# A pair-sum loop that takes in more of the next layer's work, on one Trainium2 core

## The reference

```
h   = tanh(txt_proj[:, None] + feat_proj[:, :, None] + b)
rho = h . w  + (1 - q_mask) * NEG
att = softmax(rho);  txt_h = att @ text
x   = x + tanh(g) * (tanh(txt_h . Wcw) * features + tanh(txt_h . Wcb))
```

## Time and profile before

| | us |
|---|---|
| median of 3 runs (lowest, highest) | 616.18 (615.16, 616.81) |
| the profiled execution | 613.41 |
| its span in the profile | 611.6 |
| PE busy, share of the span | 563.5, 92% |
| DVE | 445.4, 73% |
| ACT | 415.8, 68% |
| POOL | 117.0, 19% |

### The profile page before, as it was taken

How to read it: one execution, slowest core, us unless ns; L and a number is a source line. 1 busy time by engine, 2 the same in 40 slices (tenths; PEclk the granted TensorE clock), 3 DMA queues, 4 the chain that set the end, 5 groups by cost and what they waited for, 6 DMA issues and landing times.

```text
span 611.6 us, 8766 instructions
## 1 busy us (share of the span) xinstructions
PE 563.5 (92%) x3281; PEld 390.9 (64%) x3284; DVE 445.4 (73%) x684; ACT 415.8 (68%) x581; POOL 117.0 (19%) x74
## 2 busy tenths in 40 slices
PE   7999999978998999998865899999998999999997
PEld 5667887846776777776210247556655777788886
DVE  4358988768646889986968658576767836787786
ACT  4779888916754565656999976624504856988885
POOL 5400000241210000002999914200000310000000
PEclk9999999979999999999899999999999999999999
DMA  6207110200200811020000022604610110812100
GB/s 233 70 15 298 49 55 1 73 2 1 75 1 3 312 38 41 34 69 1 2 5 1 1 69 70 194 16 122 190 34 1 38 36 0 297 50 70 35 1 34
DMA packets 16782, 40.27 MB, mean 66 GB/s; under 512 B 1834, under 2 KB 6058, under 8 KB 16740
## 3 DMA queue, kind: packets, MB, share of 16 engines
q1 hardware_dynamic: 16740, 39.71, 19.5%
HBM read 39.01 MB, written 0.70 MB: 65 GB/s over the span
## 4 chain that ended last, share of the span: by engine, by line
PE 71%; DVE 13%; ACT 11%; issue 3%; POOL 1%; ACTq 0%; DVEq 0%; POOLq 0%
PE ps L680 38%; ACT work L1046 7%; PE ps L723 4%; DVE h_lo L1523 3%; PE ps L445 2%; PE ps L573 2%; PE ps L706 2%; PE ps L544 2%; PE ps L708 2%; PE ps L707 2%; PE ps L462 2%; PE ps L662 2%; PE ps L558 2%; PE ps L452 2%; PE ps L439 1%
## 5 line engine op out<-in xcount | busy, mean ns | idle before, releaser
L1523 DVE TENSOR_TENSOR h_lo<-h_act,h_hi 128x512 fp32r<-128x512 f32 (+1 forms) x136 | 120.0, 886 | 41.0 <-ACT h_hi L1083 40.4
L680 PE MATMUL ps<-n_hi,w_hi 128*128 128x512 f32 (+1 forms) x232 | 85.8, 403 | 6.8 <-DVE h_act L1500 4.3
L1083 ACT CAST h_hi<-h_act 128x1024 fp32r<-128x1024 f32 (+1 forms) x88 | 75.3, 856 | 15.3 <-PE ps L680 12.8
L680 PE MATMUL ps<-n_hi,w_lo 128*128 128x512 f32 (+1 forms) x232 | 83.1, 392 | 0.0
L680 PE MATMUL ps<-n_lo,w_hi 128*128 128x512 f32 (+1 forms) x232 | 83.0, 391 | 0.0
L1721 POOL TENSOR_TENSOR rstd<-var_eps,minus_half 128x4 f32<-128x4 f32 x16 | 17.8, 1114 | 313.5 <-DVE var_eps L1217 313.5
L680 PE MATMUL ps<-h_hi,w_hi 128*128 128x512 f32 (+1 forms) x184 | 65.6, 399 | 4.5 <-DVE h_lo L1523 4.3
L680 PE MATMUL ps<-h_hi,w_lo 128*128 128x512 f32 (+1 forms) x184 | 64.3, 392 | 0.0
L680 PE MATMUL ps<-h_lo,w_hi 128*128 128x512 f32 (+1 forms) x184 | 64.0, 390 | 0.0
L1046 ACT ACTIVATE work<-work,p_rest 128x2048 f32<-128x2048 f32 x32 | 61.4, 2000 | 1.3 <-DVE work L1388 1.3
L1755 POOL TENSOR_TENSOR work<-xc,txt 128x2048 f32<-128x2048 f32 x16 | 58.3, 3684 | 5.0 <-ACT xc L1023 4.3
(11 more groups left out here) (225 smaller groups left out, 1015.9 us busy)
## 6 DMA issues: line engine op xcount, KB each, us to landing
work<-g_rows SPq DMA_DIRECT2D x36, 512.0 KB, 6.5
w_f<-in_w SPq DMA_DIRECT2D x20, 512.0 KB, 3.5
w_f<-in_w SPq DMA_DIRECT2D x8, 544.0 KB, 3.7
work<-in_w SPq DMA_DIRECT2D x2, 512.0 KB, 4.5
work<-g_rows SPq DMA_DIRECT2D x4, 256.0 KB, 9.2
p_rest<-in_p_rest SPq DMA_DIRECT2D x1, 714.0 KB, 9.9
p_attn<-in_p_attn SPq DMA_DIRECT2D x1, 546.5 KB, 7.0
x<-in_xT SPq DMA_DIRECT2D x1, 512.0 KB, 3.7
```

The source lines that it names most:

```text
L680: mm = pe.matmul(dst[i], wap(wt, e, lo, size, rows), mv[i], start=(first and c == 0), stop=(last and c == 2))
L1083: act.copy(places(h_hi, m, step), places(h_act, m, step)).then_inc(s["hi"], 1)
L1523: dve.tensor_tensor(lo, src, hi.bitcast(F32), ALU.subtract).then_inc(s["lo"], 1)
```

## The change

- **Sums.** POOL gets the even groups from 2 to 30 (15), DVE group 0 and all odd ones (17). Group 0's sum is made in two halves of 16 features, and so is its tanh. PE makes the features of half 0 twice, into bank 2 (read by DVE) and bank 0 (copied by ACT); group 0's sum waits for the first of the two alone.
- **Mask.** The mask bias is put into the dots' bank by a PE product with the identity ahead of each half's dots; DVE's addition is gone.
- **Finish.** Both last products of the MoE before are finished by DVE at g = 3.
- **Fourth layer.** Values (all) and keys of half 0 are made in the loop by PE and copied by DVE instead of ACT; keys of half 1 move to steps 5 and 8 of the MoE, with ACT copies at its steps 19 and 22.
- **Next MoE.** Softmax, weights, update and norm (5, 0) of half 0 stand earlier in the loop. norm_high, the logits, the routing's activation (as Exp, with an addition and a reciprocal on DVE) and up(0), up(1) are in the loop, and DVE routes half 0 ahead of softmax(1). Behind the loop the order on PE, ACT and DVE is new.

The core of the diff (hunks that only renumber banks or waits are cut; of ACT's order in the MoE only the new one stands):

```diff
-        POOL_SUMS = [g for g in range(2 * B) if g % 2]
-
-        def sum_of(g, features):
+        POOL_SUMS = [g for g in range(2, 2 * B) if g % 2 == 0]
+
+        def sum_of(g, features, part=slice(0, 32)):
 
             b, f = g // 2, (g // 2) % (B // 2) * S + 32 * (g % 2)
-            return (pairs[:, g % 6].rearrange("p (f s) -> p f s", s=S), bcast(features[:, f:f + 32], 2, S), bcast(txt[:, b * S:(b + 1) * S], 1, 32))
+            count = part.stop - part.start
+            return (pairs[:, g % 6].rearrange("p (f s) -> p f s", s=S)[:, part], bcast(features[:, f + part.start:f + part.stop], 2, S),
+                    bcast(txt[:, b * S:(b + 1) * S], 1, count))
+
+        def own_sums(g):
+
+            return g + 2 - len([p for p in POOL_SUMS if p <= g])
...
             def features(t):
                 pe.wait_ge(ln["n"], 2 * 4 + t + 1)
-                pe.matmul(ps[:, FEAT[t]], l2w[:, 1], n[:, half(t)], start=True, stop=True).then_inc(x2["feat"], 1)
+                for bank in sorted({FEAT[t], FEAT_COPY[t]}, reverse=True):
+                    pe.matmul(ps[:, bank], l2w[:, 1], n[:, half(t)], start=True, stop=True).then_inc(x2["feat"], 1)
+
+            def mask_dots(t):
+
+                pe.wait_ge(in_pack["mask"], 16)
+                pe.wait_ge(consts, 2)
+                dots = ps[:, DOTS[t]].rearrange("p (f s) -> p f s", s=S)
+                pe.matmul(dots, ident, bcast(mbias[:, 1], 1, 8), start=True, stop=False)
 
             def pair_sums():
 
                 for g in range(2 * B):
-
+                    if g % B == 0:
+                        mask_dots(g // B)
                     if g == 1:
                         prepare_weighted()
                     if g == 2:
@@ -642,25 +664,35 @@
                         prepare_text(1, 4)
                     if g == 5:
                         norm_var(4, 1)
+                    if g in (6, 7):
+                        prepare_values(1, g - 6)
                     if g == 8:
                         norm_spread(4, 1)
+                    if g == 9:
+                        prepare_keys(1, 0, 0)
                     if g == 11:
                         features(1)
-                    if g in (24, 25):
-                        weights_out(0, g - 24)
+                    if g in (10, 12):
+                        prepare_values(1, 2 + (g - 10) // 2)
+                    if g == 14:
+                        prepare_keys(1, 0, 1)
...
+                    if g == 23:
+                        weights_out(0, 0)
+                        weights_out(0, 1)
+                    if g == 25:
+                        norm_mean(5, 0)
+                    if g == 26:
+                        norm_var(5, 0)
                     if g == 27:
-                        norm_mean(5, 0)
-                    if g in (26, 29):
-                        prepare_keys(1, 0, (g - 26) // 3)
+                        norm_spread(5, 0)
                     if g == 28:
-                        norm_var(5, 0)
-                    if g == 30:
-                        norm_spread(5, 0)
+                        logits(MOES[2], 0)
+                    yield g
...
+                    for g in pair_sums():
+                        if g == 29:
+                            pe.wait_ge(ln["lo"], 2 * L + 1)
+                            up(0)
+                        if g == 30:
+                            pe.wait_ge(x2["sumA"], own_sums(2 * B - 1))
+                            up(1)
+                    turn_gates((0,))
+                    up(2)
+                    out_bias(0)
+                    up(3)
                     weights_out(1, 0)
                     weights_out(1, 1)
-                    up(2)
-                    prepare_values(1, 2)
+                    up(4)
                     norm_mean(5, 1)
-                    up(3)
+                    up(5)
                     norm_var(5, 1)
-                    prepare_values(1, 3)
-                    up(4)
+                    up(6)
+                    up(7)
                     norm_spread(5, 1)
-                    up(5)
-                    pe.wait_ge(pre["vcp"], 8)
+                    up(8)
+                    up(9)
                     logits(m, 1)
-                    up(6)
-                    turn_gates((0,))
-                    up(7)
-                    up(8)
-                    out_bias(0)
+                    up(10)
                     spread_gate(0)
-                    up(9)
+                    up(11)
                     spread_gate(1)
-                    for step in range(10, m.ahead):
+                    for step in range(12, m.ahead):
...
+                    if L == 2 and step in (5, 8):
+                        prepare_keys(1, 1, (step - 5) // 3)
...
+                def first_tanh():
+
+                    for part in range(2):
+                        act.wait_ge(x2["sumA"], part + 1)
+                        dst = pairs[:, 0, 1024 * part:1024 * part + 1024]
+                        ins = act.activation(dst, dst, ACT.Tanh, bias=l2b[:, 0:1])
+                    ins.then_inc(x2["tanh"], 1)
+
+                for e in range(2):
+                    first_weights(MOES[2], e)
                 copy_features(0)
-                for e in range(4):
+                first_tanh()
+                for e in range(2, 4):
                     first_weights(MOES[2], e)
-                for g in range(2 * B):
+                for g in range(1, 2 * B):
                     if g == 4:
                         norm_square(4, 1)
                         norm_copy(4, 1)
                     if g == 13:
                         copy_features(1)
-                    if g == 28:
+                    if g == 18:
+                        softmax_exp(0)
+                    if g == 21:
+                        weights_tanh(0)
+                    if g == 26:
                         norm_square(5, 0)
                         norm_copy(5, 0)
-                    if g == 19:
-                        softmax_exp(0)
-                    if g == 23:
-                        weights_tanh(0)
-                    of_pool = len([p for p in POOL_SUMS if p <= g])
+                    if g == 29:
+                        norm_high(5, 0)
+                        first_routing()
...
+            def first_routing():
+
+                E = MOES[2].routed
+                act.wait_ge(once["logit"], 2 * 2 + 1)
+                act.activation(route_view("e", E)[:, 0:HT], ps[:, 6, 0:HT * E].rearrange("p (c e) -> p c e", e=E),
+                               ACT.Exp, scale=-1.0).then_inc(once["e"], 1)
...
+                    copy_gates(0)
                     softmax_exp(1)
                     load_table(ACT.Silu)
                     hidden(0)
+                    for e in range(4, 6):
+                        split_hi_up(m, e)
+                    hidden(1)
                     weights_tanh(1)
+                    for e in range(6, 8):
                         split_hi_up(m, e)
+                    for step in range(2, 5):
+                        hidden(step)
+                        split_hi_up(m, step + 6)
                     norm_square(5, 1)
                     norm_copy(5, 1)
+                    hidden(5)
+                    split_hi_up(m, 11)
+                    hidden(6)
+                    hidden(7)
                     norm_high(5, 1)
+                    hidden(8)
+                    split_hi_up(m, 12)
+                    hidden(9)
+                    split_hi_up(m, 13)
+                    hidden(10)
                     routing(1)
+                    for step in range(11, m.total):
                         hidden(step)
                         if step + 3 < 16:
                             split_hi_up(m, step + 3)
                         if step == 18:
                             copy_gates(1)
+                        if step in (19, 22):
+                            copy_keys(1, 1, (step - 19) // 3)
...
-            def softmax(t, between=lambda: None):
+            def softmax(t):
                 dve.wait_ge(x2["dot"], B * (t + 1))
-                link(dve.tensor_tensor(dots(t), dots(t), bcast(mbias[:, 1], 1, 8), ALU.add))
-                between()
...
+                    if g == 0:
+                        dve.wait_ge(x2["feat"], 1)
+                        dve.wait_ge(pre["txtcp"], 1)
+                        for part in range(2):
+                            dve.tensor_tensor(*sum_of(0, ps[:, FEAT[0]], slice(16 * part, 16 * part + 16)), ALU.add).then_inc(x2["sumA"], 1)
+                        continue
+                    if g == B:
+                        dve.wait_ge(x2["fb"], 2)
+                        dve.wait_ge(pre["txtcp"], 2)
+                    if g == 3:
                         finish(MOES[1], 6, 1)
-                    if g == 3:
                         finish(MOES[1], 7, 1)
...
+                    if g in (13, 15):
+                        copy_value((g - 13) // 2)
                     if g == 15:
```

(91 more changed lines are left out.)

54 lines of the change are left out of this document (12 added, 42 removed).

## The result

The changed kernel takes 622.53 us (median of 7 runs, 619.58 to 623.99), the kernel before, on the same chip, 615.93 (7 runs, 613.44 to 616.81): ratio 1.0111, 95% interval 1.0088 to 1.0135. It is 1.1% slower, and outside the range. The profiled execution took 623.06 us.

What follows compares the result with a forecast made beforehand. ACT was taken to pace the loop and PE the third MoE, with a partly idle start-up between. Terms -1.5 - 0.9 + 6.5 - 2.1 - 0.5 gave 1.5 us gained from 616.18: 614.7, range 611.6 to 617.6.

Steps and rivals of the forecast that it cites:

- The start: Start of the pair-sum loop, up to tanh 4: 1.5 us lost, with bounds of 0.5 to 2.5 lost.
- Inside the loop: From tanh 4 to the end of the last tanh: 0.9 us more, bounds +0.6 to -3.
- T: End of the loop's last tanh, 356.01 in the kernel before and forecast at 358.45.
- the rival for slower: Ahead of tanh 29: norm chain becomes the wait, deciding from 7.2 us; about 618.7 us in all, chance 0.13.
- Behind the loop: From the last tanh to the first down product: 6.5 us less than 42.9, bounds +7 to +5.
- the clock term: Behind the loop, slow clock after PE's idle of 4.6 us pushes up(3): 0.5 us lost, bounds nothing and 1.75.
- The keys put off: Two keys products of half 1 at steps 5 and 8 of the MoE, where PE is full: 2.1 us lost.
- The rival "no change": Slow clock costs 0.7 in the loop and 0.5 more behind it: 0.3 us gained, about 615.9, chance 0.20.
- the ramp: Start-up between the loop's last tanh and the first down product, forecast to take 36.85 us.
- The cover of 0.8: In the loop: features(1) done at 317.5, ACT wants them at 318.35, so ten PE insertions cost nothing.
- the rival for faster: The 2.4 us at the last tanh shrink to nothing: 3.9 gained, 4.0 with high clock, about 612.2; chance 0.21.

Runs made afterwards that it cites:

- the late POOL wait: The changed kernel with POOL's group-4 sum waiting for both finishes, 18 filling products behind the loop, and POOL's group-30 sum waiting for the update: 615.18 us, ratio 0.9986.
- finish through PSUM: The changed kernel without a further wait, DVE writing the last two experts' product back to PSUM so each add has one SBUF operand: 615.72 us, ratio 1.0002.

## Why the prediction was wrong

**The start: wrong, and this is the step that failed.** "An add, 1.29 while POOL works, with the gaps 3.8 together" took one row for the price of an add beside POOL. That row was the tail of a hold: what was left of POOL's sum at the issue (0.74), and 0.55. The price is not a property of the add but of the moment, anything from 0.69 to some 4.2 (an estimate: a whole sum of 3.62 and the 0.55). The change also took away what had limited it. Before, POOL's sum of group 5 waited for the second finish; now it has the sums of groups 2, 4 and 6 to make without a wait, and one is always in flight. The adds took 7.36 instead of 2.58, 4.78 more, and tanh 4 started 19.44 behind the feature product, where 14.89 was forecast, 4.55 more. My bound of the start (0.5 to 2.5) had only 0.69 as its other end. The sum was short by itself too: two multiplications of 0.69 and two adds of 1.29 are 3.96 without any gap, not 3.8. The rest of that paragraph held: full sum 1 at 292.14 to 294.42, 5.6 behind the feature product where 5.8 was forecast, and with the adds at 0.69 tanh 3 waited 1.08.

**Inside the loop: nearly right.** From tanh 4 to T 58.05, forecast 57.25. The 0.8 is about the third held add: the square waited 1.51 where 0.6 was forecast. The insertions on PE and DVE cost ACT nothing in this execution.

**The norm chain, the rival for slower: right size, not the cause.** From norm_mean's end (351.65 + 1.12 = 352.77) to n (359.10) are 6.33; forecast 6.3, and the rival began at 7.2. ACT waited 0.33 ahead of the Exp; forecast 0.3. The sign was that of my rival, the mechanism wasn't. It is no empty rival, though: in the profiled executions of five later kernels the clock fell to 0.88 to 0.92 between 345 and T, and ACT waited 0.92 to 1.38 ahead of the Exp.

**Behind the loop: right but for the clock.** Routing was done at T + 0.4 (forecast 0.5), up(2) started at T + 6.3 (6.2), and in the six kernels with the gap filled the first down product comes at T + 36.05 to 36.11 (forecast 36.35, ahead of the clock term). The clock term, 0.5, was 3.0 in the profiled execution and outside its bound of 1.75: I let the half rate end with out_bias, and bounded it by 3.5 us, while it held for 10 us. In the two other kernels that left the gap open it was the 0.5 forecast (T to down 36.61 and 36.64), so that it is a term that one row couldn't price.

**The keys put off: right.** 1.7 measured, 2.1 forecast.

**The rival "no change"** (low clock in the ramp eats the cover of features(1)) did not decide, but in two of the kernels whose adds were mended (the late POOL wait, and finish through PSUM) it did occur, at 2.39 of ACT. The cover of 0.8 was too thin to be priced at nothing.

**The sum and its ends.** My bounds add up to a loss of 2.6 us and, with the clock's own bound, 4.35, not 2, and the rival for faster to 4.4 gained with the clock high, not 4.0. None of them covers the 6.6 lost.

Together from the feature product on: 5.35 of the start and the loop, 2.25 of the ramp, -0.4 of the keys and 1.5 of the clock in the untouched end are the 8.7 between 323.8 and 332.49. In the kernel with all three adds mended and the gap filled 6.8 are won behind T, less 1.1 that T comes later and 1.7 of keys. That is 4.0 by these marks, and 2.5 with the 1.5 of low clock behind its last down product; its median is 2.4 under the kernel before (0.4% by its ratio). With the keys moved too it is 0.7 to 1%.

## What to carry to other kernels

When an instruction's duration in a row is not the usual one of its shape, ask what it waited for inside before using it as a price: lay its start and end beside the other engines' instructions. Before moving a DVE instruction with two SBUF operands next to a busy POOL, give it a PSUM operand, or a place where POOL waits anyway, and watch that the change doesn't remove that wait. A gap made on PE is worth filling with work that has to be done somewhere, here 1.7 us of it, ahead of filling it with dummies.

## What the runs showed of the hardware

- A DVE add of two 128x512 SBUF operands is held to 0.55 us behind the end of the POOL sum in flight (fifteen adds in eight kernels, 1.03 to 4.09 long), and a POOL sum that begins meanwhile takes 4.07 instead of 3.62: each side waits for the other. With one operand in PSUM it is 0.69 beside a running POOL, and POOL loses nothing.
- DVE's own sums (one operand in PSUM, one in SBUF) were 2.28 throughout, beside POOL or not.
- Behind the same gap of 4.67 us on PE the granted clock was 0.50 for 10 us in the changed kernel and 0.83 in two others that left it open; it was 1.00 in the kernels that filled it with 18 dummies.
- The low clock comes and goes between executions and kernels where the code is the same. The stretch behind the last down product took 152.0 to 152.1 us in six of the twelve profiled kernels and 153.5 in the other six. The windows of the changed kernel and, behind them, of the kernel before show it, each for the first 10 us of that stretch:

```profile
467.80:477.80 10.00, 8.82 (x62) 6.07 (x63) 6.34 (x7) 3.82 (x7) 1.01 (x1) 0.83 0.01 2
```

```profile
459.60:469.60 10.00, 8.74 (x71) 5.19 (x76) 6.54 (x8) 4.36 (x7) 1.01 (x1) 1.00 0.01 2
```

The same work has 0.83 in the one and 1.00 in the other, and the stretch is 1.5 us longer. What decides between them stays open. It is of the size of the differences between some of these kernels, so those were judged by the intervals and by the marks, not by one profile.
